# Moving a third of the next batch's neighbourhood attention ahead of the routed mixture, and one of its steps behind each tile, in a decoder of two layers

## The reference, cut to what matters

```
x = ln(x + nearby_attention(x))          # 16 heads of 8, keys within 3 tokens, 7 offsets
x = ln(x + gate(x, ctx))                 # rho = w . tanh(ctx@Ws + x@W + b), softmax over 77 keys
                                         # w_s, b_s = tanh(att @ ctx @ Wc.T); w_s * x + b_s
x = ln(x + routed_mixture(x))            # 8 experts, top 2, silu(g) * u @ down
x = ln(x + top32_attention(x))           # one head, only the 32 largest scores of a row
x = ln(x + cross_attention(x, ctx))      # 77 keys
x = ln(x + gelu_mixture(x))              # shared expert + 8 experts, top 2 weights
```

## Time and profile before

| what | us |
|---|---|
| median of 3 runs (lowest to highest) | 936.6 (934.32 to 937.72) |
| the profiled execution's own time | 937.64 |
| its span in the profile | 935.8 |

### The profile page before, as it was taken

How to read it: one execution, slowest core, us unless ns; L and a number is a source line. 1 busy time by engine, 2 the same in 40 slices (tenths; PEclk the granted TensorE clock), 3 DMA queues, 4 the chain that set the end, 5 groups by cost and what they waited for, 6 DMA issues and landing times.

```text
span 935.8 us, 10819 instructions
## 1 busy us (share of the span) xinstructions
PE 665.7 (71%) x3444; PEld 435.9 (47%) x3444; DVE 473.2 (51%) x1420; ACT 423.8 (45%) x759; POOL 140.0 (15%) x138
## 2 busy tenths in 40 slices
PE   4478419886787929786788929886788929914586
PEld 1211116652245926662235926663245928803576
DVE  3678425631665645631675645631674634428444
ACT  1078305447475405447475405447485405401242
POOL 2100131103000141103000141103001130030000
PEclk8679758989799969979798969979798969957679
DMA  8024020001000030001000030001000011000000
GB/s 278 0 91 168 1 78 21 12 12 35 0 3 1 1 90 22 12 13 34 1 3 0 1 89 22 12 12 32 2 3 1 1 53 38 27 26 0 1 0 12
DMA packets 27253, 28.26 MB, mean 30 GB/s; under 512 B 5048, under 2 KB 22464, under 8 KB 26944
## 3 DMA queue, kind: packets, MB, share of 16 engines
q1 hardware_dynamic: 25152, 23.38, 7.9%
q0 software_dynamic: 2048, 4.20, 1.5%
HBM read 19.51 MB, written 8.06 MB: 29 GB/s over the span
## 4 chain that ended last, share of the span: by engine, by line
PE 39%; ACT 15%; DVE 13%; issue 10%; POOL 7%; DMA 4%; POOLq 0%; DVEq 0%; ACTq 0%
ACT a_big L986 9%; PE bank L897 5%; PE bank L779 4%; PE bank L770 3%; POOL x_rows L1666 3%; POOL b_big L1675 3%; PE bank L761 2%; PE bank L762 2%; PE bank L763 2%; PE bank L613 2%; PE bank L832 2%; PE bank L812 2%; PE bank L599 1%; PE bank L697 1%; PE bank L601 1%
## 5 line engine op out<-in xcount | busy, mean ns | idle before, releaser
L697 PE MATMUL bank<-a_big,score_pad 128*32 128x512 f32 x616 | 147.8, 615 | 7.3 <-ACT a_big L1126 5.8
L986 ACT ACTIVATE a_big<-a_sum,txt_cols 128x512 f32<-128x512 f32 x231 | 144.9, 715 | 0.8 <-PE bank L697 0.7
L1442 DVE TENSOR_TENSOR b_big<-bank,b_big 128x256 f32<-128x256 f32 x120 | 50.2, 420 | 104.1 <-ACT b_big L1033 96.6
L697 PEld LDWEIGHTS bank<-a_big,score_pad 128*32 128x32 f32 x616 | 30.1, 109 | 104.5 <-ACT a_big L986 56.1
L897 PEld LDWEIGHTS bank<-rw_sb,b_big 128*128 128x128 f32 x576 | 70.5, 194 | 2.8
L897 PE MATMUL bank<-rw_sb,b_big 128*128 128x128 f32 x576 | 71.1, 277 | 0.0
L1097 ACT ACTIVATE b_big<-bank,cols_sb 128x512 f32<-128x512 f32 x72 | 48.5, 687 | 45.4 <-PE bank L601 44.4
L779 PEld LDWEIGHTS bank<-down_sb,b_big 128*128 128x128 f32 x480 | 64.9, 198 | 8.6 <-issue 3.4
L779 PE MATMUL bank<-down_sb,b_big 128*128 x480 | 65.5, 281 | 2.8 <-ACT b_big L1022 2.2
L751 PE MATMUL bank<-const_sb,b_big 128*128 128x128 f32 x60 | 18.7, 311 | 66.2 <-DMA b_big<-x_rows 61.4
L1033 ACT ACTIVATE b_big<-bank 128x256 f32<-128x256 f32 x120 | 45.9, 382 | 43.5 <-PE bank L763 40.9
(11 more groups left out here) (249 smaller groups left out, 1229.5 us busy)
## 6 DMA issues: line engine op xcount, KB each, us to landing
b_big<-gup SPq DMA_DIRECT2D x8, 512.0 KB, 6.0
y_rows<-b_big SPq DMA_DIRECT2D x60, 64.0 KB, 1.5
down_sb<-down SPq DMA_DIRECT2D x1, 2048.0 KB, 7.7
b_big<-x_rows SPq DMA_DIRECT2D x4, 512.0 KB, 4.4
rw_sb<-rw SPq DMA_DIRECT2D x1, 1152.0 KB, 10.0
a_T<-x_T SPq DMA_DIRECT2D x4, 256.0 KB, 2.6
a_tok<-x_tok SPq DMA_DIRECT2D x4, 256.0 KB, 3.1
b_big<-rw SPq DMA_DIRECT2D x2, 512.0 KB, 3.5
```

Of the source, the lines that this page charges most:

```text
L697: last = mm(P[2][32 * j:32 * j + 32, :], score_pad[:, 31 - i:63 - i], ring[k % RING], start=(i == 0), stop=(KCOL * (i + 1) + j >= KEYS))
L986: act(ring[k % RING], a_sum[:, 0:S], ACT.Tanh, bias=txt_cols[:, c:c + 1])\
L1442: tt(gated[i % 2][:, h * 256:(h + 1) * 256], P[3 + h][:, 256:512], silu_sb[i % 2][:, h * 256:(h + 1) * 256], ALU.mult).then_inc(gated_read ...
```

## The change

1. The seven products all go to DVE; POOL only adds the bias to `a_tok`, in a function of its own (`attended_input`), one batch earlier in its queue.
2. The attention's steps are split: the first eight (`FIRST_STEPS`) are issued in the mixture of the batch two before: project and value behind expert 7, the others at the mixture's end; for batch 1 they stand behind batch 0's `positions`. The others (`STEPS_AT`) come one to a tile, after both halves of it, in tiles 0 to 10.
3. The tanh rounds: none between tiles. 0 to 5 behind the tiles, 6 to 14 in the top attention (6, 7 to 10, 11 to 14), 15 to 19 in the cross attention; PE's ranges are the same as ACT's.
4. The gate's tail moves up: `gate_rows` and the transpose before the last transpose of `cross_attention`'s result, shift and exponential before the mixture, sums before its weights, apply at expert 0, normalise at 1, transposes and logits at 3, rank at 4, positions and slots at 5. The logits and positions use bank 1 instead of bank 2.

```diff
-PE_AT = {"project": 1, "value": 2, "score": 6, "to_tokens": 8, "to_rows": 13, "spread": 16, "output": 20,
-         "turn": 23, "feature": 24}
-ACT_AT = {"project": 1, "value": 2, "rows": 7, "exp": 10, "to_rows": 12, "turn": 24, "feature": 24}
-DVE_AT = {"project": 0, "product": 2, "shift": 9, "probability": 11, "rest": 14, "spread": 15, "sum": 18,
-         "output": 21, "normalise": 21}
-GATE_AT = (24, 26, 28, 29)
-GATE_S3_END = 8
-GATE_S4 = (8, 14, 16)
-GATE_S5 = (16, 17, 18)
+FIRST_STEPS = ("project", "value", "product", "score", "rows", "to_tokens", "shift", "exp")
+STEPS_AT = {0: ("probability",), 1: ("to_rows", "rest"), 2: (("spread", 0),), 3: (("spread", 1),),
+            4: (("spread", 2),), 5: (("spread", 3),), 6: ("sum",), 7: ("output",), 8: ("normalise",),
+            9: ("turn",), 10: ("feature",)}
+ROUNDS_AT = {"mixed": (0, 6), "scores": (6, 7), "pair0": (7, 11), "pair1": (11, 15), "cross": (15, 17),
+             "shifted": (17, 18), "last": (18, KROW)}
...
                             turn_h(i - 1)
                         if h == 1 and i >= 2:
                             down_mm(i - 2)
-                        if ahead:
-                            attend_nearby(b + 1, n, True)
-                            if n in SCORE_AT:
-                                gate_scores(b + 1, SCORE_AT.index(n), SCORE_AT.index(n) + 1)
+                    if ahead:
+                        for s in STEPS_AT.get(i, ()):
+                            attend_nearby(b + 1, s, True)
...
-                    if u == 7 and ahead:
+                    if u == 3 and ahead:
                         turn_x2(b + 1)
-                    if u == U - 1 and ahead:
                         logits_x2(b + 1)
+                    if u == 5 and ahead:
+                        positions(b + 1)
+                    if u == 7 and b + 2 < B:
+                        attend_nearby(b + 2, "project", True)
+                        attend_nearby(b + 2, "value", True)
                 down_mm(U - 1)
-                if ahead:
-                    positions(b + 1)
+                if b + 2 < B:
+                    attend_nearby(b + 2, "score", True)
+                    attend_nearby(b + 2, "to_tokens", True)
...
             def gelu_mixture(b, ahead):
+                if ahead:
+                    gate_exp(b + 1)
                 turned(b, 3)
-                if ahead:
-                    gate_rows(b + 1)
+                route_exp(b, 1)
...
-                for o in range(POOL_PROD):
-                    if s == DVE_AT["product"] + o:
-                        if o == 0:
-                            eng.wait_ge(qkv_ready, 3 * b + 2)
+                if s == "product":
+                    eng.wait_ge(qkv_ready, 3 * b + 2)
+                    for o in range(OFFS):
                         tt(prod[o], a_q[:, :], a_k[:, o:o + S], ALU.mult).then_inc(prod_ready, 1)
...
             def gelu_mixture(b, ahead):
                 halves_b(b)
                 route_b(b)
                 if ahead:
-                    gate_shift(b + 1)
+                    gate_sums(b + 1)
+                weigh_b(b)
                 per = U + 1
                 for u in range(U):
-                    if u == EXP_AT:
-                        weigh_b(b)
-                    if u == U - 1 and ahead:
-                        rank_x2(b + 1)
+                    if ahead:
+                        if u == 0:
+                            gate_apply(b + 1)
+                        if u == 1:
+                            normalise_a(b + 1, 2)
+                        if u == 4:
+                            rank_x2(b + 1)
+                        if u == 5:
+                            place_x2(b + 1)
+                    if u == 7 and b + 2 < B:
+                        attend_nearby(b + 2, "project")
+                    if u == 8 and b + 2 < B:
+                        attend_nearby(b + 2, "product")
                     eng.wait_ge(down6_psum, U * b + u + 1)
...
-                if ahead:
-                    place_x2(b + 1)
-                norm_b(b, 4, part6_ready, per * b + per)
+                statistics_b(b, 4, part6_ready, per * b + per)
+                if b + 2 < B:
+                    attend_nearby(b + 2, "shift")
+                normalise_b(b, 4)
```

189 lines of the change are left out of this document (102 added, 87 removed).

## The result

The change makes the kernel faster: 868.96 us median (868.54 to 870.32) against 936.6, ratio 0.9285 with a 95% interval of 0.9253 to 0.9317. The profiled execution took 868.54 us, its span is 866.7 (before: 937.64 and 935.8).

What follows compares the result with a forecast made beforehand. No engine's total bounds the kernel (PE busy 71%), but which wait ends last in each stage. Terms -73 - 13.9 + 17 + 3 - 2 = -69 from 937.6 gave 869, stated as 870 us; range 850 to 898.

Steps and rivals of the forecast that it cites:

- Tiles, -73: Tiles overlapping the next batch's attention: 58 us in place of 83.0, three times 24.5 saved; bounds 54 and 70 us.
- the 4 us of waits for probability, to_rows and output: In the tiles: 3 us where to_rows waits for probability's wide DVE operations, and 1 us at output.
- Tanh, +17: Attentions: top +4.1 and cross +1.5 from moved tanh rounds, 3 x 5.6; six rounds behind the tiles hidden; bounds 0 and 3 x 8.
- some 0.8 us: Top attention: ACT twice waits this long for PE's last score matmul and transposes.
- half hidden: Cross attention: one more tanh round ahead of its transpose, half covered by the statistics, costing +1.5 us.
- Mixture, +3, with positions 2.4 and project and value 7.4: Mixture: gate's tail 3 x 1 us, positions 3 x 0.8, project and value 3.7 us of PE in batches 0 and 1.
- Mixture's end to `x_hi`, 10.6 us twice and 5.4 once: Gap ahead of the tiles, 18.1 before: 10.6 us bounded by the new chain twice; 12.7 us less ahead of the last batch.
- First batch, +4 and -2: Batch 0: chain ahead of its tiles ends some 4 us behind the load, +4; seven products alone release PE earlier, -2.
- rival 4: Tiles: draining so deep that they gain nothing; at 3 us per step tiles of 87 us, kernel 954 us; chance 0.03.
- the drained tiles (1 and 4): Steps stall the in-order engines in the tiles; rival 1: 1.5 us per step, tiles 70 us, kernel 905, chance 0.12.
- The stretched scatter (2): Gap ahead of the tiles: scatter stretched or late by DVE's work or POOL's queue, gap stays 18 us, kernel 897; chance 0.08.
- The clock (3): Gather's gap and behind: tanh matmuls may keep PE at 2.4 GHz, up to -3.7 us three times, kernel 858; chance 0.07.

Runs made afterwards that it cites:

- e9_same: The changed kernel run once more, unaltered; 863.09 us, ratio 0.9201.
- e3_lag: Changed kernel, but PE scores one tanh round less than ACT has made, from the top attention's first pair to the last round; 847.48 us.
- e4_rounds: Changed kernel with eight tanh rounds behind the tiles instead of six, and three instead of four in each pair of the top attention; 839.85 us.
- e6_late: Changed kernel, but ahead of the last batch alone positions and places are made behind the mixture again; 875.53 us.
- e5_early: Changed kernel with DVE's seven products issued before the mixture's sum over tile 7 instead of behind it; 856.99 us.
- e10_mid: Changed kernel with all attention steps in the tiles, the first of a tile's two between its halves, the second behind it; 898.01 us.

## Why the prediction was right

The forecast was 870 us in a range of 850 to 898, and 868.96 was measured. That it came so close is luck: two of its terms were wrong by about as much in opposite directions.

- *Tiles, -73.* Measured -85.1. The sign and the mechanism (a silu wait "far below 29 us": 9.9) were right, the size was not: 52.0 us, not 58, and outside the 56 to 60 that it gave. The step that failed is the 4 us of waits for probability, to_rows and output: they did not come, PE idles for 1.0 us in all. The 48.0 us of the tiles alone run 2.4 us past their end (from the first `x_hi` to the end of the last transposed tile's copy they took 45.6), but the 82.5 that the new tiles were taken from is 2.2 above the marks' mean of 80.3 too, so this cancels. By that end the tiles with steps take 52.1 us, 6.5 more than those alone in e9_same (45.5): the 6 us of PE time were nearly right.
- *Tanh, +17.* Measured 31.4 + 1.7, less the 1.6 us for the late `b_T` that the prediction had in the mixture, three times: 28.3, above its bound of 24. The mechanism was right: ACT at DVE's edge, a wait behind the search near 8 us (9.61), one round more and PE on ACT's round. Two sizes failed: "some 0.8 us" for PE's lag, twice a batch, is 1.7 us at each pair, as e3_lag shows by removing it, and the cross attention's round is not "half hidden" but costs its 2.5 us. The tanh behind the tiles were hidden, as it said; they end 6.1 us before the first transpose, not 3 to 4. What it did not see is that this was the place for two more rounds (e4_rounds).
- *Mixture, +3, with positions 2.4 and project and value 7.4.* 12.8 forecast; measured 8.3 and the 4.8 of the late `b_T`, 13.1.
- *Mixture's end to `x_hi`, 10.6 us twice and 5.4 once.* Measured 11.7, 12.1 and 5.6, and 9.4, 10.7 and 5.2 in e9_same. Right, with its reason: the new chain bounds in batches 0 and 1 and the load in the last, and e6_late shows that the slots in the mixture do it. But the products need not have stood behind DVE's sum (e5_early).
- *First batch, +4 and -2.* Measured +0.1. The exponential came 1.2 us earlier (24.96 for 26.12). Ahead of batch 0's tiles the new chain took 10.6 us from the first product to the end of exp, not 12.6, and ended 1.2 us behind the first transposed rows, not 4 behind the load.

The terms with their errors: tiles -12, tanh +11, first batch -2, mixture and gap +3. One sum beside them is off: rival 4 counts its tiles from 83.0 us, where the term counts from 82.5 (58 + 24.5), so it would cost from 81.1 us on, and tiles of 87 would give 955.

Of the rivals, the drained tiles (1 and 4) did not come about; e10_mid shows what they would have looked like, steps that chain from engine to engine between the halves. The stretched scatter (2) did not either: 0.96 us an issue beside DVE's products, but for single issues of 1.20 to 1.50 us beside the products ahead of batch 0's tiles, in nine of the eleven profiles that have products there. The rule on two-port modes of the Trainium skill, SBUF — State Buffer, "Who interferes with whom", is not touched by these products, which have two tensors as inputs; no run here put a long operation of the other kind beside the scatter. The clock (3) gave nothing in the changed kernel: 0.67 from the first `b_T` to the tanh, against 0.75 before,

```profile
450.82:461.00 10.18, 9.07 (x28) 3.89 (x28) 3.90 (x10) 4.20 (x9) 0.00 (x0) 0.75 0.01 2
```

but it is a real term: with two rounds more it gave 2.6 us a batch.

## What to carry to other kernels

When work is moved between stages, price the place it leaves and the place it goes to by what is idle there: the same tanh round cost 3.1 us in a full tile, 2.5 us ahead of an edge, and less than nothing in a gap whose idleness also cost the clock (two rounds moved there gave 7.5 us a batch, of which 4.9 are their own time). Where engines hand a ring of buffers on, try to let the consumer end a stage one round behind the producer (13.5 us here), so that the next stage's first operation does not stand behind a round that is just being made. And look, for each step that is placed early, at what stands ahead of it in its engine's queue: the head start here was worth nothing until the products were moved past one sum.
